# Building two edge-count tables with indirect adds: clears in batches, eight groups compared ahead of the row statistics, spread trash places, and table sums interleaved with the aggregation

## What is computed

```python
agg = jax.ops.segment_sum(h[src], dst, num_segments=N)
deg = jax.ops.segment_sum(jnp.ones((src.shape[0],), h.dtype), dst, num_segments=N)
mean_agg = agg / jnp.maximum(deg, 1.0)[:, None]
out = mean_agg @ Wl + bl + h @ Wr
```

## Time and profile before

| | |
|---|---|
| median of 3 runs | 3154.77 us (3154.65 to 3165.74) |
| the profiled execution, its own time | 3173.5 us |
| its span in the profile | 3171.7 us |
| PE busy / DVE busy / POOL busy, share of the span | 73% / 41% / 28% |
| mean granted clock of PE | 0.862 |
| indirect adds on POOL | 224 to `at_counts`, 350.1 us busy; 192 to `odd_counts`, 303.4 us |
| chain that ended last, by engine | PE 52%, DVE 19%, ACT's queue 15%, issue 9% |

### The profile page before, as it was taken

One profiled execution on the slowest core, in us unless ns is written; L12 is line 12 of the kernel. 1 busy time (PEld: TensorE's weight loads), 2 busy tenths in 40 slices (PEclk: granted clock), 3 DMA queues, 4 the chain that ended last, 5 costly groups with the idle time before them and its releaser, 6 DMA issues.

```text
span 3171.7 us, 40580 instructions
## 1 busy us (share of the span) xinstructions
PE 2328.0 (73%) x14330; PEld 1817.1 (57%) x14330; DVE 1309.7 (41%) x2752; ACT 409.8 (13%) x822; POOL 896.2 (28%) x643
## 2 busy tenths in 40 slices
PE   1122100058849999988997977999899985999997
PEld 1111100036536766766773455888688875888886
DVE  6599999954422011111116834113311775111111
ACT  0011000000005100004102213000200001322322
POOL 2588888887810000000002210000100000333332
PEclk6556555579979999998997979999999987999999
DMA  9833333368560799991351000444244424666665
GB/s 351 297 44 51 48 47 53 40 207 269 145 220 14 170 183 216 216 222 44 95 189 34 0 0 1 152 147 147 70 135 146 151 68 137 191 190 177 191 190 136
DMA packets 288667, 426.94 MB, mean 135 GB/s; under 512 B 166211, under 2 KB 223834, under 8 KB 288512
## 3 DMA queue, kind: packets, MB, share of 16 engines
q1 hardware_dynamic: 104959, 297.03, 29.2%
q10 hardware_dynamic: 109696, 106.77, 13.7%
q0 software_dynamic: 73936, 22.14, 8.1%
HBM read 307.61 MB, written 100.96 MB: 129 GB/s over the span
## 4 chain that ended last, share of the span: by engine, by line
PE 52%; DVE 19%; ACTq 15%; issue 9%; ACT 2%; DVEq 1%; DMA 1%; POOL 0%; SPq 0%
ACTq L714 11%; PE ps L1823 8%; PE ps L1824 8%; PE ps L1582 8%; PE ps L1901 7%; PE ps L1892 7%; DVE late L983 6%; PE ps L1517 4%; DVE ring L983 4%; ACTq L631 1%; PE ps L1600 1%; PE ps L1774 1%; PE ps L1671 1%; PE ps L1574 1%; ACTq L622 1%
## 5 line engine op out<-in xcount | busy, mean ns | idle before, releaser
L1823 PE MATMUL ps<-harena,ring 128*128 128x257 f16 x2500 | 555.3, 274 | 3.7 <-DVE harena L1255 2.7
L1824 PE MATMUL ps<-harena,ring 128*128 128x256 f16 x2500 | 555.0, 273 | 0.0
L1582 PE MATMUL ps<-ring,harena 128*128 128x320 f16 (+1 forms) x4000 | 540.4, 297 | 1.4 <-ACT tarena L669 0.8
L1582 PEld LDWEIGHTS ps<-ring,harena 128*128 128x128 f16 x4000 | 393.0, 98 | 145.4 <-issue 3.1
L518 POOL DMA_INDIRECT at_counts<-harena x224 | 350.1, 1563 | 159.1 <-issue 75.8
L983 DVE SCALAR_TENSOR_TENSOR late<-ring,ps 128x1024 f16<-128x1024 f32 x312 | 378.9, 1275 | 2.7 <-issue 2.7
L518 POOL DMA_INDIRECT odd_counts<-harena x192 | 303.4, 1580 | 61.6 <-issue 57.9
L1823 PEld LDWEIGHTS ps<-harena,ring 128*128 128x128 f16 x2500 | 242.8, 97 | 43.1 <-DVE harena L1299 3.7
L1824 PEld LDWEIGHTS ps<-harena,ring 128*128 128x128 f16 x2500 | 243.1, 97 | 32.5
L1606 PE MATMUL ps<-ident,sc 128*1 128x128 f32 x8 | 2.1, 364 | 331.8 <-DVE sc L938 331.8
L1901 PE MATMUL ps<-ring,harena 128*128 128x256 f32 x1024 | 229.4, 382 | 8.8 <-ACT harena L847 7.9
(11 more groups left out here) (345 smaller groups left out, 2648.9 us busy)
## 6 DMA issues: line engine op xcount, KB each, us to landing
ring<-at_counts SPq DMA_DIRECT2D x150, 800.0 KB, 6.6
ring<-L_ffn_W SPq DMA_DIRECT2D x64, 1024.0 KB, 5.3
ring<-ad_counts SPq DMA_DIRECT2D x50, 800.0 KB, 4.2
ring<-key_rows SPq DMA_DIRECT2D x52, 512.0 KB, 3.7
at_counts<-tarena ACTq DMA_DIRECT2D x5, 4000.0 KB, 38.7
odd_counts<-tarena ACTq DMA_DIRECT2D x5, 4000.0 KB, 38.8
xrows<-odd_counts SPq DMA_DIRECT2D x25, 800.0 KB, 10.3
at_counts<-ring ACTq DMA_DIRECT2D x25, 800.0 KB, 8.5
```

The costliest lines, as they stand in the source:

```text
L1582: ins = M(ps[:, 2 * f + h, 0:c], part[:, t, (2 * k + f) * P:(2 * k + f + 1) * P], chunk[q][:, s, h * HB:h * HB + c], start=(t == 0 and par ...
L1823: M(ps[:, i, 0:F + 1], lhs, hh[:, t, 0:F + 1], start=(t == 0), stop=False)
L1824: ins = M(ps[:, i, 0:F], lhs, hl[:, t, :], start=False, stop=(t == T - 1))
```

## The change

1. **Clears.** The trash places of both tables are cleared first, then block 0 of both tables, then, after the small weights, block b of both tables for b = 1 to 4, each pair issued once everything before it has landed.
2. **POOL's start.** POOL no longer waits for a whole table. DVE works out in which block the last destination of the first eight groups lies (`row_block`, `first_block`), PE transposes it, and POOL loads a value from it and waits for as many clears: 64 (both trash regions and block 0 of both tables) if they all lie in block 0. All clears are awaited only before group 8.
3. **Turns.** Even groups go to `at_counts` and odd ones to `odd_counts` from the first group on, each waiting for the group before in its own table; the waits after each of the first four groups are gone, and so are the two at the end.
4. **Trash places** lie 64 elements (128 bytes) apart instead of one element (2 bytes): `SPREAD`.
5. **Order of DVE.** Groups 0 to 7 are compared before the row statistics; the rounds after them are 11 instead of 12. SP loads x straight after the first four key rows, without a wait for clears.
6. **Sums.** For blocks 1 to 3 the sums of chunks 0 and 1 come ahead of `aggregated` of the block before, those of chunks 2, 3 and 4 inside it (after the scaling, after the first addition, and at its end). Block 4's five sums stay behind `aggregated(3)`.

```diff
-            pool.wait_ge(zeroed, 16 * (NB + 1))
             def add_group(g, table, added):
                 pool.wait_ge(idx_ready, g + 1)
+                if g >= 2:
+                    pool.wait_ge(added, g // 2 * GROUP)
...
-            for g in range(LOOK):
-                add_group(g, at_flat, even_added)
-                pool.wait_ge(even_added, (g + 1) * GROUP)
-            pool.wait_ge(zeroed, 2 * 16 * (NB + 1))
-            for g in range(LOOK, NG, 2):
-                pool.wait_ge(even_added, (g + LOOK) // 2 * GROUP)
+            pool.wait_ge(idx_ready, 1)
+            cleared = pool.value_load(release[:, 3, 0:1], min_val=64, max_val=64 + 32 * (NB - 1))
+            pool.wait_ge(zeroed, cleared)
+            for g in range(0, NG, 2):
+                if g == FIRST_GROUPS:
+                    pool.wait_ge(zeroed, 32 * (NB + 1))
                 add_group(g, at_flat, even_added)
-                if g > LOOK:
-                    pool.wait_ge(odd_added, (g - LOOK) // 2 * GROUP)
                 add_group(g + 1, odd_flat, odd_added)
...
+            for flat in (at_flat, odd_flat):
+                act.dma_start(flat[ASIZE:ASIZE + GE * SPREAD, :]..., zeros16[:, 0:GE * SPREAD // P]...).then_inc(zeroed, 16)
+            clear(at, 0)
+            clear(odd, 0)
             (small weights)
-            act.wait_ge(zeroed, 16 * (NB + 1))
+            for b in range(1, NB):
+                act.wait_ge(zeroed, 32 * (b + 1))
+                clear(at, b)
+                clear(odd, b)
...
-            sp.wait_ge(zeroed, 16 * (NB + 1))
             sp.dma_start(xrows[:, 0:T - 1, :], x[0:(T - 1) * P, :].rearrange("(t p) d -> p t d", p=P)).then_inc(x_in, 16)
...
-            o.mark(nc.gpsimd.iota(etrash_i, pattern=[[P, GQ]], base=ASIZE, channel_multiplier=1))
+            o.mark(nc.gpsimd.iota(etrash_i, pattern=[[P * SPREAD, GQ]], base=ASIZE, channel_multiplier=SPREAD))
...
+            o.mark(V.tensor_reduce(row_block, eflt[:, 3, :], AX.X, ALU.max))
+            step(V.tensor_reduce(first_block, ps[0:1, 1, 0:2 * FIRST_GROUPS], AX.X, ALU.max))
+            step(V.tensor_scalar(release[:, 3, 0:1], first_block, 32.0, 64.0, ALU.mult, ALU.add))
...
-            edges_of(0, True)
+            edges_of(0, 0)
+            edges_of(0, 1)
...
-                    for b in range(NB):
-                        if b:
-                            aggregated(b - 1, HB)
-                        for q in range(NB):
-                            sum_tables(b, q)
+                    for q in range(NB):
+                        sum_tables(0, q)
+                    for b in range(NB - 1):
+                        if b == NB - 2:
+                            aggregated(b, HB)
+                            for q in range(NB):
+                                sum_tables(NB - 1, q)
+                            break
+                        for q in (0, 1):
+                            sum_tables(b + 1, q)
+                        def next_sums(n):
+                            sum_tables(b + 1, 2 + n)
+                        aggregated(b, HB, next_sums)
```

57 lines of the change are left out of this document (31 added, 26 removed).

## The result

| | before | after |
|---|---|---|
| median of the runs, us | 3155.75 (3154.65 to 3165.74, 4 runs) | 3107.61 (3103.96 to 3126.72, 4 runs) |
| ratio | | 0.9852, 95% interval 0.9818 to 0.9885 |
| profiled execution: own time, span, us | 3173.5, 3171.7 | 3106.31, 3104.5 |

The change takes 48.1 us off the median. The forecast was 3102 us with a range of 3089 to 3122.

What follows compares the result with a forecast made beforehand. The last block's start was taken to wait for GpSimd's series of indirect adds. Start 12.3, waits 26.0 and tail 14.1 sum to 52.4 us, and 3154.8 - 52.4 gives 3102 us; range 3089 to 3122.

Steps and rivals of the forecast that it cites:

- POOL's start: GpSimd's first add, decided by its indices and not the clears, comes at 53.6 instead of 65.92: -12.3 us.
- The waits of the first four groups: GpSimd's waits for landed adds after each of the first four groups go and nothing comes back: -26.0 us.
- The series: GpSimd's adds from first to last, less those waits, stay at 790.9 us, with the same loads beside them.
- Steps 5 and 6 of the change are worth nothing by themselves: VectorE's new order and the interleaved sums gain nothing, as GpSimd's adds cover VectorE and TensorE by 33 us.
- The tail: Landing after the last odd add falls from 16.4 to 2.3 us with trash places spread: -14.1 us.
- The 0.4 us that were to be left: Part of the tail kept if sharing a 512-byte stretch costs: three queued trash places at 0.12 us each.
- Rival A: The tail after the last add stays at 16.4 us; time 3116 us; chance 12%.
- DVE and PE: VectorE and TensorE cost 0 while GpSimd covers them: first block at about 635, gap before the last about 33 us.
- No stall for x: Moving x's load ahead was to stall VectorE for 0 to 5 us, waiting for group 4's key row.
- Clears: All clears land at 139 to 159 us, before GpSimd needs them ahead of group 8 at 172.
- rival B: GpSimd waits before group 8 for clears or indices, costing 5 to 15 us: 3107 to 3117 us; chance 8%.
- Rival C: GpSimd's stops of 9.34 and 3.4 us fall elsewhere or vanish, 13 us less: 3089 us; chance 6%.

Runs made afterwards that it cites:

- experiment 4: Changed kernel with GpSimd again waiting, after each of the first four groups, until that group has landed: 3140.08 us.
- experiment 3: Changed kernel with the old order of sums, all five sums of a block behind the work on the block before: 3099.3 us.
- experiment 11: Changed kernel with four groups compared ahead of the row statistics instead of eight: 3144.38 us, one run.
- experiment 2: Changed kernel with neighbouring trash places 2 bytes apart again instead of 128: 3128.13 us.
- experiment 9: Changed kernel with each sum of 3200 elements cut into four TENSOR_TENSOR of 800: 3099.34 us.
- experiment 7: The kernel before, unchanged, profiled a second time: 3169.39 us; fifteen other executions in the same session have a median of 3157.57 us.
- experiment 1: The changed kernel run again without any edit, for the spread: 3107.07 us.
- experiment 10: Changed kernel with the old order of sums, each sum in four pieces, and the slice weights' folding put behind the first four groups: 3095.55 us.
- experiment 8: Changed kernel with trash places 16 bytes apart instead of 128: 3111.03 us.
- experiment 12: Changed kernel, its own order of sums kept, with each sum in four pieces and the slice weights' folding behind the first four groups: 3099.2 us.

## Why the prediction was right

The forecast for the last block's start was 857.5 us and it came at 856.47; the forecast for the whole was 3102 and it is 3107.6. The mechanism was right: the front waited for GpSimd's adds, and its start, its waits and its tail were what the change shortened. That the start of the block was met within 1 us is partly luck: 2.4 us more won at the first add and 2.5 us lost in the series cancel. Step by step:

- **POOL's start, -12.3: it was -14.7.** The chain was right (indices decide, clears don't). The reduction and its tiny steps cost 0.69 + 0.16 + 0.14 us, inside the 1.2 taken with the transpose. The indices were there at 49.34 instead of 52.5, mostly because the edges reached VectorE at 8.53 us, where they had come at 11.19 before, which I had no reason to move; the loaded value and its waits took 1.85 us where I had taken 1.1.
- **The waits of the first four groups, -26.0: confirmed**, and experiment 4 shows that such waits pass to the end in full.
- **The series, kept at 790.9: 793.4.** This is the step where the reasoning was wrong although the size is small. I wrote that "the same loads will run beside the same adds". They don't: with the old order of the sums the series is 785.9 (experiment 3). Of its slow adds I had only said that they lie in the time of the chunk loads; they stand next to sums, in the kernel before too (VectorE, then GpSimd):

```profile
677.06 1.82 DVE L1069 TENSOR_TENSOR ring<-ring,xrows 128x3200 f16<-128x3200 f16 x1 [4.85 <-DMA xrows<-odd_counts]
```

```profile
677.63 2.68 POOL L518 DMA_INDIRECT odd_counts<-harena  x1 [0.30 <-issue]
```

  This add ends 1.43 us behind the sum. And the total stayed near 790.9 by luck: against the first profile of before the stops fell from 12.9 to 4.3 us and the excess rose from 8.9 to 18.0.
- **"Steps 5 and 6 of the change are worth nothing by themselves": refuted twice.** Step 6, the interleaved sums, costs 8 us (experiment 3). I costed it on VectorE and PE alone and gave it 0 because both had cover; its price fell on GpSimd, whose adds are held by sums and stop beside the loads; how much each of the two took isn't shown. Step 5, the order of VectorE, is what the batches of step 1 stand on: with four groups ahead GpSimd waits 37.4 us (experiment 11). I had it as a matter of x landing and overlooked what queues behind the clears on ScalarE. Had I asked that of the added waits, I should have seen a stall of 7.47 us for ScalarE in the earlier trace rows already.
- **The tail, -14.1: it was -14.8**, and by experiment 2 the trash places account for all of it: 18.3 us came back there, 0.15 us per place where I estimated 0.12. The 0.4 us that were to be left if sharing a stretch of 512 bytes costs did not show: the tail is 1.6 us at 128 and at 16 bytes, where four and 32 places share such a stretch. Rival A did not come.
- **DVE and PE:** first block at 633.2 (forecast 635), gap before the last block 31.0 (33). Blocks of 47 us are 45.6 and 45.9, but the first takes 56.2: its products (L1626) run beside the next block's sums and last 11.88 us after a wait of 6.65. No stall for x.
- **Clears** at 157 us, inside 139 to 159, and GpSimd passes group 8 at 170.38 without a wait: rival B did not come.
- **Rival C**, the series without POOL's stops, came in its condition and not in its time: the stops of 9.34 and 3.4 us shrank to 2.71 and 2.04, but the excess took as much back. Experiments 3 and 9 show that 8 of its 13 us were to be had, by the old order of the sums or by cutting them.

The 5 us between 3102 and 3107.6 don't come from the front, where the forecast gain was 1.0 us too small. The forecast took its shift off the median of before, 3154.8; less 909.9 for the front and 1.8 around the span that leaves 2243 us behind it, where both profiles of after have 2248.0. Part of the 5 us may lie in the value that it started from: later medians of before are 3155.75 to 3160.27, and from the 3157.57 of experiment 7 the same shift gives 3105. What makes up the rest stays open.

## What to carry to other kernels

When a step is moved on an engine that has time, cost it on the engine that has none: beside which of its instructions will it lie now, and what do both reach for. For GpSimd's indirect adds that means every VectorE instruction with two inputs in SBUF, by its length. Cutting such instructions helped here (experiment 9); keeping one operand in PSUM looks promising, since no add is held beside the comparisons, which do that, but no run tries it on the sums. When waits are added to a queue, list everything behind them in that queue, however small: here one 0.23 us square root decided how much comparing had to be done ahead.

## What was not expected of the hardware

- An indirect add that is held by a VectorE instruction with two SBUF inputs ends 1.42 us behind that instruction's end, within 0.01 us, in all 20 cases of the changed kernel's sums. An add that starts ahead of the instruction isn't held, and in experiment 1 one that starts 0.01 us behind it isn't either (1.55 us); that sum takes 1.87 us instead of 1.82. Between the pieces of a cut instruction it can get in, but twice in experiment 10 it did not and stood 3.91 and 4.39 us.
- The opcode does not decide it: 1.82 us of TENSOR_TENSOR cost 0.9 us of GpSimd, 3.49 us of SCALAR_TENSOR_TENSOR 2.3, and SCALAR_TENSOR_TENSOR with one operand in PSUM nothing.
- 122 adds to places 2 bytes apart land late, by 18.3 us or 0.15 us each, as if they went one after the other; 16 bytes apart they don't.
- Beside the loads of the tables GpSimd stops, for 2.7 to 17.3 us in all. The part in front of a group waits for landed adds (up to 7.67 us, experiment 8); the part inside a group (up to 11.79 us, experiment 12) has no wait in the program, and its cause stays open.
